# A graph attention layer: two contiguous blocks in each slot of the ring, and the loads of dst issued by ScalarE

## The reference

```python
h_src, h_dst = x[src], x[dst]
e = leaky_relu(concat([h_src, h_dst, ef]) @ W_att + b_att, 0.01)
ex = exp(e - segment_max(e, dst)[dst])
alpha = ex / segment_sum(ex, dst)[dst]
z = segment_sum(alpha[:, None] * (concat([h_src, ef]) @ W_ne), dst)
out = relu(concat([x, z]) @ W_out)
return layernorm(x + out)
```

## Time and profile before

| | us |
|---|---|
| median of 3 timed runs | 5012.17 |
| lowest, highest | 5008.59, 5013.94 |
| the profiled execution, whole program | 4990.13 |
| its span, first to last instruction | 4988.3 |

### The profile page before, as it was taken

One profiled execution on the slowest core, in us unless ns is written; L12 is line 12 of the kernel. 1 busy time (PEld: TensorE's weight loads), 2 busy tenths in 40 slices (PEclk: granted clock), 3 DMA queues, 4 the chain that ended last, 5 costly groups with the idle time before them and its releaser, 6 DMA issues.

```text
span 4988.3 us, 64221 instructions
## 1 busy us (share of the span) xinstructions
PE 2010.8 (40%) x9870; PEld 1926.7 (39%) x9871; DVE 2579.2 (52%) x4868; ACT 2315.7 (46%) x4121; POOL 2978.3 (60%) x3149
## 2 busy tenths in 40 slices
PE   1444444434343334443434333434333433343346
PEld 0334444433333333333433333433333333343346
DVE  5555455555554555555555555545555555555556
ACT  1455555444444444444444444444444444444444
POOL 6566666666666666666666666656666666666651
PEclk9666666666666666666666666666666666666666
DMA  5444444444444444444444444444444444454441
GB/s 111 122 130 126 128 129 132 128 129 129 127 127 128 130 129 130 130 127 124 131 128 127 127 130 130 130 129 128 126 129 127 129 129 130 123 136 128 126 129 53
DMA packets 759570, 628.92 MB, mean 126 GB/s; under 512 B 608412, under 2 KB 608796, under 8 KB 759332
## 3 DMA queue, kind: packets, MB, share of 16 engines
q1 hardware_dynamic: 646164, 519.51, 36.2%
q0 software_dynamic: 100096, 102.60, 11.1%
q10 hardware_dynamic: 13072, 4.80, 0.5%
HBM read 621.58 MB, written 4.81 MB: 126 GB/s over the span
## 4 chain that ended last, share of the span: by engine, by line
issue 31%; another core or an unknown queue 17%; ACT 17%; DVE 15%; DVEq 10%; ACTq 7%; PE 1%; POOL 0%
ACT zb L508 4%; ACT psE L507 4%; DVE prod L619 3%; DVE u L623 3%; DVEq L741 2%; ACTq L513 2%; ACT acc L471 2%; DVE um L728 2%; ACT pT L461 2%; DVE acc L682 2%; ACT psS L499 2%; DVE e L689 1%; DVEq L708 1%; ACT ebias L502 1%
## 5 line engine op out<-in xcount | busy, mean ns | idle before, releaser
L365 POOL DMA_INDIRECT V<-in_x_dram,srcs x3128 | 2953.4, 944 | 1883.4 <-PEq L892 951.2
L851 PE MATMUL psT<-ident,e 128*128 128x128 f32 x3136 | 757.9, 421 | 2593.2 <-ACT pT L461 1249.6
L851 PEld LDWEIGHTS psT<-ident,e 128*128 128x128 f32 x3136 | 615.5, 219 | 2664.2 <-issue 2399.5
L857 PE MATMUL psG<-V,pT 128*128 x6288 | 1237.3, 379 | 13.4 <-DVE acc L682 11.2
L857 PEld LDWEIGHTS psG<-V,pT 128*128 128x128 f32 x6288 | 1232.3, 299 | 15.3 <-issue 15.2
L461 ACT COPY pT<-psT 128x512 f32<-128x512 f32 x784 | 434.0, 579 | 1348.6 <-remote 1301.4
L619 DVE TENSOR_TENSOR prod<-V,psM 128x1024 f32<-128x1024 f32 x391 | 477.6, 1221 | 828.0 <-issue 827.9
L728 DVE CUSTOM_DVE_ANT_0 um<-ubc,psS 128x1024 f32<-128x1024 f32 x391 | 476.5, 1219 | 617.1 <-issue 315.6
L623 DVE TENSOR_REDUCE u<-prod 128x8 f32<-128x1024 f32 x391 | 477.0, 1220 | 62.5 <-issue 22.4
L689 DVE TENSOR_TENSOR e<-zb,psE 128x1024 f32<-128x1024 f32 x392 | 475.5, 1213 | 10.6 <-issue 8.0
L499 ACT ACTIVATE psS<-dbc,nbias 128x1024 f32<-128x1024 int32 x391 | 437.0, 1118 | 12.8
(11 more groups left out here) (95 smaller groups left out, 656.3 us busy)
## 6 DMA issues: line engine op xcount, KB each, us to landing
ubc<-scores SPq DMA_DIRECT2D x391, 512.0 KB
dbc<-in_dst_dram SPq DMA_DIRECT2D x390, 512.0 KB
V<-in_edge_attr_dram SPq DMA_DIRECT2D x390, 256.0 KB
V<-in_x_dram,srcs POOLq DMA_INDIRECT x3128
scores<-u SPq DMA_DIRECT2D x391, 4.0 KB
srcs<-in_src_dram SPq DMA_DIRECT2D x390, 4.0 KB
out_dram<-y SPq DMA_DIRECT2D x12, 256.0 KB
xt<-in_x_dram ACTq DMA_DIRECT2D x6, 448.0 KB
```

What stands on the lines that cost most here:

```text
L365: nc.gpsimd.indirect_dma_start(V[0:n, s, j, 0:F], None, x[:, :], bass.IndirectOffsetOnAxis(ap=srcs[0:n, s, j:j + 1], axis=0)).then_inc(h_i ...
L851: last = nc.tensor.transpose(psT[:, i, j * P:(j + 1) * P], e1[:, :].rearrange("q (p j) -> q j p", j=J)[:, 4 * i + j, :], ident[:, :])
L857: last = nc.tensor.matmul(psG[:, 0:AW], pT[:, i, j * P:(j + 1) * P], V[:, bass.ds(sv, 1), 4 * i + j, :].rearrange("p a f -> p (a f)"), sta ...
```

## The change

The layout of V changes. A slot is 1056 columns: a block of eight times [x row, one], XW = 65 columns each, and from column EF_AT = 528 a block of the eight ef rows one behind the other, 2 KB in each partition. PE's moving operand is a view of two pieces of 65 columns: the second starts with an ef row, and its 65th column, the first of the row behind it (or one cleared column behind the eighth), is multiplied too and goes into a column of `acc` that nobody reads. AW becomes 130, and the sum of the ones is column F. DVE's product becomes two instructions, and the sum runs over two axes. POOL's scaling at the end (L395) leaves out the columns between.

The load of dst leaves SP's step. ACT issues the load of tile t + 2 behind the window of tile t, into the place of `dbc` that its Square of tile t has read, with a wait for that Square. SP still loads dst of the first two tiles and of the last. ACT's last turn is written out, so that its last two tiles issue none.

```diff
-VW = 2 * F + 1
-AW = 2 * F + 1
+XW = F + 1
+EF_AT = 528
+ONE_PAST = EF_AT + 8 * F
+SLOT = 1056
+AW = 2 * XW
...
-        V = sb("V", [P, RING, J, VW])
+        V = sb("V", [P, RING * SLOT + (J - 1) * XW + 2 * (EF_AT - J + 1) - SLOT])
+        Vs = V[:, 0:RING * SLOT].rearrange("p (s w) -> p s w", w=SLOT)
+        Vx = Vs[:, :, 0:J * XW].rearrange("p s (j w) -> p s j w", w=XW)
+        Ve = Vs[:, :, EF_AT:EF_AT + J * F].rearrange("p s (j f) -> p s j f", f=F)
...
             def load_ef(t, s):
-                sp.dma_start(V[:, s, :, F:2 * F], (ef[bass.ds(t * ST, ST), :]).rearrange("(p j) f -> p j f", j=J)).then_inc(ef_in[s], 16)
+                sp.dma_start(Ve[:, s, :, :], (ef[bass.ds(t * ST, ST), :]).rearrange("(p j) f -> p j f", j=J)).then_inc(ef_in[s], 16)
...
                 store_scores(n, r)
-                load_dst(n, r)
                 spread_scores(n, r)
...
-                    nc.gpsimd.indirect_dma_start(V[0:n, s, j, 0:F], None, x[:, :],
+                    nc.gpsimd.indirect_dma_start(Vx[0:n, s, j, 0:F], None, x[:, :],
...
-            def supertile(k, s, ahead):
+            def supertile(k, s, ahead, next_dst=True):
...
                 if ahead:
                     act.load(coming, trip[0:1, bass.ds(2 * t + 2, 2)])
+                if next_dst:
+                    act.wait_ge(sq_done, act.snap(g) - 1)
+                    act.dma_start(dbc[:, s % 2, :], edge_rows(dst, t + 2).rearrange("(a e) -> a e", a=1).broadcast_to((P, ST))).then_inc(d_in[s % 2], 16)
...
-            with act.Fori(YT, TURNS) as k:
+            with act.Fori(YT, TURNS - 1) as k:
                 for s in range(RING):
                     supertile(k, s, True)
+            for s in range(RING):
+                supertile(TURNS - 1, s, True, s < RING - 2)
...
             def edge_product(s):
-                return nc.vector.tensor_tensor(prod[:, :].rearrange("p (j k f) -> p j k f", k=2, f=F), V[:, s, :, 0:2 * F].rearrange("p j (k f) -> p j k f", k=2),
-                                               wa_v.unsqueeze(1).broadcast_to((P, J, 2, F)), ALU.mult)
+                for k, rows in enumerate((Vx[:, s, :, 0:F], Ve[:, s, :, :])):
+                    last = nc.vector.tensor_tensor(prod[:, k * J * F:(k + 1) * J * F].rearrange("p (j f) -> p j f", f=F), rows,
+                                                   wa_v[:, k:k + 1, :].broadcast_to((P, J, F)), ALU.mult)
+                return last
 
             def edge_score(i):
-                return nc.vector.tensor_reduce(u[:, i, :], prod[:, :].rearrange("p (j f) -> p j f", f=2 * F), AX, ALU.add)
+                return nc.vector.tensor_reduce(u[:, i, :], prod[:, :].rearrange("p (k j f) -> p j k f", k=2, f=F), AXY, ALU.add)
...
                     last = nc.tensor.matmul(psG[:, 0:AW], pT[:, i, j * P:(j + 1) * P],
-                                            V[:, bass.ds(sv, 1), 4 * i + j, :].rearrange("p a f -> p (a f)"),
+                                            V[:, bass.ds(sv + XW * (4 * i + j), 2 * (EF_AT - 4 * i - j))].rearrange("p (k w) -> p k w", k=2)[:, :, 0:XW],
                                             start=(i == 0 and j == 0), stop=(i == 1 and j == 3))
```

More of the change, by code:

```diff
@@ L25 @@
 AX = mybir.AxisListType.X
+AXY = mybir.AxisListType.XY
 P = 128
@@ L98, in graph_attention @@
         accv = acc[:, :].rearrange("p (b f) -> p b f", f=AW)
+        accz = acc[:, :].rearrange("p (b k w) -> p b k w", k=2, w=XW)
         node = sb("node", [P, NB + 1, 3])
-        V = sb("V", [P, RING, J, VW])
+        V = sb("V", [P, RING * SLOT + (J - 1) * XW + 2 * (EF_AT - J + 1) - SLOT])
+        Vs = V[:, 0:RING * SLOT].rearrange("p (s w) -> p s w", w=SLOT)
+        Vx = Vs[:, :, 0:J * XW].rearrange("p s (j w) -> p s j w", w=XW)
+        Ve = Vs[:, :, EF_AT:EF_AT + J * F].rearrange("p s (j f) -> p s j f", f=F)
         srcs = sb("srcs", [P, RING, J], U32)
@@ L297, in _ @@
                 store_scores(n, n % 2)
-                load_dst(n, n % 2)
                 spread_scores(n, n % 2)
@@ L331, in _ @@
                     sp.wait_ge(v_free[0], TURNS)
-                    sp.dma_start(V[0:PL, 0, :, F:2 * F], ef[full * ST:E, :].rearrange("(p j) f -> p j f", j=J)).then_inc(ef_in[0], 16)
+                    sp.dma_start(Ve[0:PL, 0, :, :], ef[full * ST:E, :].rearrange("(p j) f -> p j f", j=J)).then_inc(ef_in[0], 16)
             store_scores(full, full % 2)
@@ L394, in octet @@
                 pool.wait_ge(z_turned, 2 * o + 2)
-                nc.gpsimd.tensor_tensor((e1, zb)[par][:, 0:w * P].rearrange("p (b f) -> p b f", f=P), accv[:, bass.ds(8 * o, w), 0:P],
-                                        rl[:, bass.ds(8 * o, w)].unsqueeze(2).broadcast_to((P, w, P)), ALU.mult).then_inc(z_ready, 1)
+                nc.gpsimd.tensor_tensor((e1, zb)[par][:, 0:w * P].rearrange("p (b k f) -> p b k f", k=2, f=F), accz[:, bass.ds(8 * o, w), :, 0:F],
+                                        rl[:, bass.ds(8 * o, w)].unsqueeze(2).unsqueeze(3).broadcast_to((P, w, 2, F)), ALU.mult).then_inc(z_ready, 1)
             octets(pool, octet, 0)
@@ L524, in _ @@
                         y_pair(YS * k + s)
-            with act.Fori(YT, TURNS) as k:
+            with act.Fori(YT, TURNS - 1) as k:
                 for s in range(RING):
                     supertile(k, s, True)
+            for s in range(RING):
+                supertile(TURNS - 1, s, True, s < RING - 2)
             act.wait_ge(y_ready, PAIRS + 2)
             nc.scalar.copy(y1[:, NB:NB + 2, :].rearrange("p b f -> p (b f)"), y_out).then_inc(y_copied, 1)
-            supertile(TURNS, 0, False)
+            supertile(TURNS, 0, False, False)
             rescale(act.snap(g))
@@ L571, in _ @@
             nc.vector.memset(dnone[:, :], -P).then_inc(dnone_set, 1)
-            nc.vector.memset(V[:, :, :, VW - 1:VW], 1.0)
+            nc.vector.memset(Vx[:, :, :, F:XW], 1.0)
+            nc.vector.memset(Vs[:, :, ONE_PAST:ONE_PAST + 1], 0.0)
             nc.vector.memset(node[:, :, 2:3], UNSEEN)
@@ L769, in _ @@
             dve.wait_ge(merged, dve.snap(g))
-            step(nc.vector.tensor_scalar(rl[:, :], accv[:, 0:NB, 2 * F], TINY, None, ALU.max))
+            step(nc.vector.tensor_scalar(rl[:, :], accv[:, 0:NB, F], TINY, None, ALU.max))
             nc.vector.reciprocal(rl[:, :], rl[:, :]).then_inc(all_merged, 1)
@@ L864, in window @@
                 G = pe.snap(g)
-                sv = pe.snap(slot[2], min_val=0, max_val=RING - 1)
+                sv = pe.snap(slot[2], min_val=0, max_val=(RING - 1) * SLOT)
                 pe.wait_ge(pt[0], G)
@@ L884, in supertile @@
                 windows = pe.snap(count, min_val=1, max_val=NB)
-                pe.reg_mov(slot[0], s)
+                pe.reg_mov(slot[0], s * SLOT)
                 with pe.Fori(0, windows):
```

## The result

The changed kernel took 4989.14 us (median of 5 runs, 4988.3 to 4993.26) against 5011.65 of the kernel before (5 runs, 5008.59 to 5013.94): a ratio of 0.9959, 95% interval 0.9946 to 0.9973. It is faster by 22 us; I had forecast 5060 and slower.

A forecast was written before the change was run, and what follows sets the result against it. The prediction took a round trip between engines, gathers to agg_done to gathers, as the bound. Ring +46, tail +5 and start -3 made +48 us on the 5012.17 median: 5060 us, slower, range 4890 to 5145.

The forecast's parts named there:

- the share of 0.18: Ring: fraction of added chain delay that reaches the tile time, from the first seven turns; 0.12 us a tile, +46 us.
- part 4: Edge feature loads: 1024 runs of 256 B become 128 of 2 KB; nothing in the steady state.
- The round trip: Ring: period of 12.34 us is 9.67 of gathers, 1.87 to agg_done and 0.80 until POOL starts.
- Part 1: ScalarE's issue of the dst load, ahead of nbias and Square: 0.53 us later after agg_done (0.34 to 0.92).
- Parts 2 and 3: SP loses the dst issue and the 512 KB move behind agg_done: nothing, at best scores 0.3 us earlier.
- Rival B: Between last gather and agg_done: removing dst traffic shortens POOL's wait by 0.1 to 0.5 us a tile; chance 21%.
- rival C: Small runs hold the loop: period falls towards POOL's 10 us, half way 1.2 us a tile, 4560; chance 6%.
- Part 5: DVE's split product +0.15 us, two-axis sum nothing (at worst 0.3 us), wider merge, rescale and PE matmuls 0.03 us.
- Part 6: Ends: tail's seven bare windows at 0.68 us, +5 us; start's quicker first feature loads, -3 us (0 to -5).

The follow-up runs named there:

- e2: Kernel before with only the dst loads moved to ScalarE, old layout: 4945.37 us, ratio 1.0027 against the kernel before.
- e3: Kernel before with only the new layout, SP still issuing the dst loads: 4905.01 us, ratio 0.9947 against the kernel before.
- e13: New layout alone but ef rows 65 columns apart, so loads stay 1024 runs of 256 B: ratio 0.9997 against the kernel before, chip with waits.
- e4: Kernel before plus one unused 128x1024 copy on ScalarE ahead of nbias in every tile: 4938.18 against 4934.51 us, ratio 1.0009.
- e18: Kernel before plus two unused 128x1024 copies on ScalarE ahead of nbias in every tile: 4952.48 against 4933.85 us, ratio 1.0037.
- e14: Kernel before, old layout, with SP issuing the dst load last in its step: ratio 0.9993 against the kernel before, chip with waits.
- e17: New layout with SP issuing the dst load last in its step, ScalarE none: 4909.39 against 4933.85 us of the kernel before, ratio 0.9952.
- e16: Kernel before with PE's eight matmuls ahead of the window's eight transposes: 5199.87 against 4932.22 us, ratio 1.0565, chip with waits.
- e7: Kernel before, old layout, with SP issuing the dst load last in its step: ratio 1.0004 against the kernel before, chip without waits.
- e5: New layout alone but ef rows 65 columns apart, so loads stay 1024 runs of 256 B: ratio 1.0004 against the kernel before, chip without waits.

## Why the prediction was wrong

Two terms of the sum failed. The chain's delay times the share of 0.18 was priced at +46 us and the fewer runs of part 4 at nothing. The runs showed +11 us for the moved load (e2) and -29.5 for the layout (e3), all of it from the fewer runs (e13).

**The round trip.** That agg_done follows the end of a gather batch and that no engine off POOL sets the ring was right for the traced chip: e4 and e18 delay ACT by 0.95 and 1.9 us and the ring of their traces doesn't move. But I took what one chip does for a property of the kernel; on another chip the same program has no such wait at all.

**Part 1, ScalarE's issue, and the share of 0.18.** The size was right in an ordinary tile, 0.35 us of issue and the Square 0.57 us later (2.47 against 1.90) for my 0.53, and within my bounds on average (0.86). The step that failed is the share. From turns with 0.49 us more work on ACT and 0.09 us more a tile I took that the one causes the other, +46 us. 1.9 us of pure delay cost 19 us in all (e18), and none of them shows in the ring; a share of 0.18 would have made it 130 in the ring alone. The first seven turns also have two more PE instructions and a wait between ACT and PE in seven tiles of ten, as I noted in brackets and then put aside. The direct cost of the moved load is 11 us (e2), by a way that stays open.

**Parts 2 and 3, SP's side.** Right: SP's relief and the time of the transfer are worth nothing (e14 0.9993, e17 against e3). Rival B falls with them.

**Part 4, the fewer runs.** Here is the sign. I put it at nothing, since the DMA engines were busy for half of the time and DVE doesn't wait for the features. Measured 29.5 us (e3), and 0.05 to 0.08 us a tile in the traces. It is rival C's mechanism, of which I only priced a size of 1.2 us a tile, fifteen times too much or more, and gave it 6%. A small effect of it had no place in my cases. The Trainium skill, "DMA: Bandwidth & Descriptors", section "Why small descriptors are slow", says that each packet and descriptor carries a fixed overhead, so that small ones cost the DMA engines time. The traces agree: the packets of SP's queue took 36.8% of the 16 engines' span in e13 and 33.8% in e3, for the same 519.51 MB. But nothing here waits for the load itself, and POOL's gathers take the same 946 ns in e3 and e13; the gain is in the wait for agg_done. How the time of the packets gets there no run shows. On the chip without waits POOL sets the pace. Whether 2 KB runs gain anything there wasn't run.

**Part 5, DVE and PE.** The product costs what I worked out, 1.29 us for the pair instead of 1.22 (the two overlap in part; I had 1.37). Hidden, as said (e13).

**Part 6, the ends.** The first three feature loads are issued in 1.54 us, not 6.07, and the tail's tile is 8.30 instead of 8.21 us:

```profile
11.19 1.54 SPq L259 DMA_DIRECT2D V<-in_edge_attr_dram  x3
...
4848.02 1.22 DVE L702 TENSOR_TENSOR e<-zb,psE 128x1024 f32<-128x1024 f32 x1
...
4856.32 1.22 DVE L702 TENSOR_TENSOR e<-zb,psE 128x1024 f32<-128x1024 f32 x1
```

The issue gives back 4.5 of the 5 us that I expected, but they don't reach the loop: the first e starts at 65.57 instead of 67.23, the eleventh at 229.61 instead of 227.76. And the tail costs 7 x 0.09 = 0.6 us, not 5. All of the 0.09 is the product's, for e3 and e13, where ScalarE issues nothing, have 8.30 too. The chain over ACT is not bare in the tail, as I had taken it to be: in e18 a tile there takes in 1.1 of 1.9 us.

**The range.** It held the time, 4989 within 4890 to 5145; what failed is the direction. The chances gave 0.49 to slower, against 0.29, on the strength of one comparison within the trace.

## What to carry to other kernels

A share read from a natural experiment in a trace is worth only as much as the list of what else differs there; a delay put in on purpose costs one run and gave about 0 where the comparison gave 0.18. Where a loop waits on POOL's gathers, look for what loads the core's DMA path rather than for the length of the chain: fewer and longer runs in an unrelated load gave 0.5%, while 1.9 us more on ScalarE in every tile cost 0.4%. Time such a kernel on more than one chip: the same program differed by 23% between them. And a signal that comes earlier may be used to run more gathers in a row, which can cost more than it saves (as the timeline of e16 reads).

## What the runs showed of the hardware

- One program takes 4023 us on one chip and 4935 us on another, with the same 944 ns for a gather. Nearly all of the difference is in waits between gathers: in one kernel traced on both (e7 and e14) the spans are 4023.9 and 4928.3 us, and POOL's idle time ahead of its gathers is 955.7 and 1822.3, which makes 867 of 904. At the start of another such pair (e5 and e13) a tile takes 8.6 us on the one and up to 38.5 on the other.
- The number of runs of an ordinary load, 1024 of 256 B or 128 of 2 KB for the same 256 KB, changes the waits between gather batches by 0.05 to 0.08 us a tile on the chips with waits, though the load's own landing is waited for by nobody.
- In the ordinary tiles shown, a DMA issue took its engine 0.31 to 0.35 us (SP's L248, L254 and L259, ACT's L521; SP's L264 once 0.01), and 0.56 with 1024 runs; in a run of sixteen gathers 0.70 to 0.73.
- Two DVE products of 128x512 on the heels of each other take 1.29 us, one of 128x1024 1.22.
- What on the chip is shared between POOL's indirect DMAs and the other engines' signals, and why only some chips show it, no run here tells.
